# Four graph layers on one core: the value products stand ahead of the ring step in TensorE's program

## The reference

```python
# layers 0 and 1: one head; layer 2: eight heads, with types of edges
e = leaky_relu(s_src[:, :, None] + s_dst[:, None, :]);  e = where(adj > 0, e, NEG_BIG)
h_prime = einsum('bij,bjf->bif', softmax(e), h)          # the "value product"
...
# layer 3: for each pair of nodes a sum over 64 features
s = u[:, :, None, :] + v[:, None, :, :];  s = where(s > 0, s, ALPHA * s)
e = einsum('bijf,f->bij', s, a[:, 0])
h_prime = einsum('bij,bjf->bif', softmax(where(adj > 0, e, NEG_INF)), hp)
```

## Time and profile before

| | |
|---|---|
| median of three runs | 8730.86 us (8719.59 to 8737.53) |
| the profiled execution: its time | 8735.48 us |
| its span, first to last instruction | 8733.7 us |
| busy share of PE, DVE, ACT, POOL | 90%, 87%, 85%, 18% |
| mean granted TensorE clock | 0.975 of full speed |

### The profile page before, as it was taken

One profiled execution on the slowest core, in us unless ns is written; L12 is line 12 of the kernel. 1 busy time (PEld: TensorE's weight loads), 2 busy tenths in 40 slices (PEclk: granted clock), 3 DMA queues, 4 the chain that ended last, 5 costly groups with the idle time before them and its releaser, 6 DMA issues. The chain is left out here.

```text
span 8733.7 us, 176152 instructions
## 1 busy us (share of the span) xinstructions
PE 7856.0 (90%) x64968; PEld 3583.3 (41%) x64968; DVE 7563.2 (87%) x10853; ACT 7430.4 (85%) x8671; POOL 1535.9 (18%) x582
## 2 busy tenths in 40 slices
PE   4789999898989989999898898989999899898998
PEld 2535344353443534334343343534435344353442
DVE  4789888888889888898888898888888888988888
ACT  3688898988889888898888888889898898988888
POOL 0310304012040220302104030030301304012000
PEclk8999999999999999999999999999999999999999
DMA  3626344362443625335253352534526344362430
GB/s 86 162 56 140 78 108 113 73 144 66 112 104 83 142 64 115 96 87 139 65 122 97 84 135 59 126 91 96 124 58 143 77 108 112 76 143 67 109 83 19
DMA packets 519909, 864.90 MB, mean 99 GB/s; under 512 B 91938, under 2 KB 157474, under 8 KB 518946
## 3 DMA queue, kind: packets, MB, share of 16 engines
q1 hardware_dynamic: 518946, 852.41, 41.5%
HBM read 76.25 MB, written 4.19 MB: 9 GB/s over the span
## 5 line engine op out<-in xcount | busy, mean ns | idle before, releaser
L1134 ACT ACTIVATE work<-v,ucol 128x1024 f32<-128x1024 f32 x3757 | 4059.8, 1141 | 468.9 <-PE psum L879 466.6
L879 PE MATMUL psum<-work,pick 128*32 128x512 f32 x32768 | 3956.7, 609 | 342.5 <-DVE work L1471 208.4
L1471 DVE TENSOR_SCALAR work<-v,ucol 128x1024 f32<-128x1024 f32 x4435 | 3410.9, 823 | 204.4 <-PE psum L879 181.7
L879 PEld LDWEIGHTS psum<-work,pick 128*32 128x32 f32 x32768 | 938.2, 110 | 2601.7 <-issue 2238.1
L1281 DVE CUSTOM_DVE_ANT_0 work<-psum,work 128x1024 f32<-128x1024 f32 x1280 | 1542.5, 1205 | 320.0 <-ACT work L992 292.1
L1309 DVE STREAM_TRANSPOSE work<-work 128x1024 f32<-128x1024 f32 x1280 | 1582.7, 1237 | 56.9 <-DMA work<-work 56.2
L992 ACT ACTIVATE work<-psum,beta 128x1024 f32<-128x1024 f32 x1024 | 1138.9, 1112 | 429.8 <-PE psum L754 382.9
L1001 ACT ACTIVATE work<-work,least 128x1024 f32<-128x1024 f32 x1280 | 1463.2, 1143 | 18.9 <-DVE least L1281 18.8
L792 PEld LDWEIGHTS psum<-work,vw 128*64 128x64 f32 x16384 | 877.4, 137 | 613.2 <-issue 603.0
L792 PE MATMUL psum<-work,vw 128*64 128x128 f32 x16384 | 1118.8, 279 | 8.4 <-DMA work<-work 8.4
L750 PE MATMUL psum<-mask_next,ident_b 128*128 128x512 bf16 x2560 | 783.7, 388 | 337.0 <-DVE least L1281 306.1
(11 more groups left out here) (158 smaller groups left out, 5191.8 us busy)
## 6 DMA issues: line engine op xcount, KB each, us to landing
work<-work SPq DMA_DIRECT2D x2560, 256.0 KB, 4.6
adj_in<-in_adj SPq DMA_DIRECT2D x128, 512.0 KB, 3.6
tile3T<-blocks SPq DMA_DIRECT2D x512, 128.0 KB, 2.7
mask<-mask_next SPq DMA_DIRECT2D x128, 256.0 KB, 3.8
x_in<-in_x SPq DMA_DIRECT2D x16, 256.0 KB, 4.7
xT_both<-in_xT SPq DMA_DIRECT2D x16, 256.0 KB, 5.8
out<-yout SPq DMA_DIRECT2D x16, 256.0 KB, 2.6
work<-in_WqT SPq DMA_DIRECT2D x1, 128.0 KB
```

The source lines that it names most:

```text
L879: mm = pe.matmul(score3[32 * q:32 * q + 32, cols], pick[:, 15 - kk:47 - kk], ring[u % RING][q][:, cols], start=(kk == 0), stop=(kk == 15), ...
L1134: ins = act.activation(ring[u % RING][q], v3[:], ACT.Relu, bias=ucol[:, 4 * T + q, kk:kk + 1])
L1471: ins = dve.tensor_scalar(ring[u % RING][q], v3[:], ucol[:, 4 * T + q, kk:kk + 1], 0.0, ALU.add, ALU.max)
```

## The change

In PE's program the value product of a slot is taken out of `ahead` and called before the ring step. Nothing is added or removed, and the other engines' programs are as they were.

```diff
-            def ahead(a, it, s):
+            def products(a, it, s):
                 if s in PV_AT:
                     k, half = PV_AT[s]
                     if half is None:
                         pv_pair(a, it, k)
                     else:
                         pv_heads(a, it, k, half)
+
+            def ahead(a, it, s):
                 if s == 2:
                     column(a, it, 0)
...
                     if more and s in Q_AT:
                         make_q(g + 1, it, Q_AT[s])
+                    if more:
+                        products(g + 1, it, s)
                     if kk is not None:
                         ring_step(g, 16 * T + kk)
                     if s == 1:
...
                     make_q(0, first, Q_AT[s])
+                products(0, first, s)
                 ahead(0, first, s)
```

## The result

The change makes the kernel slower: 8781.32 us, the median of 5 runs (8768.48 to 8791.93), against 8732.98 us for the kernel before on the same chip (5 runs, 8719.59 to 8737.93). The ratio is 1.0052, with a 95% interval of 1.0037 to 1.0067. That is +48 us where +66 us was forecast, or 3.2 us a pass instead of 4.4. The profiled execution took 8777.45 us.

The account below looks back on a forecast made before the run. The prediction took a PE-DVE chain as the bound: a tile's last ring step, DVE's top read and queue, then PE waiting. Terms of 1.88 + 1.0 + 1.03 + 0.5 = 4.4 us, times 15, gave 66 us: 8799 us, range 8755 to 8830.

Parts of the forecast that it names:

- The last step of the sum: Shift from 8801 us, based on the profiled execution, to the median of runs, 4.6 us lower; given as 8799.
- Slot 15, 1.88 us: P0 ahead of R15 delays the top read; DVE's full queue passes 1.88 us a pass on to R27.
- a rival in which longer waits lower PE's clock: Added waits before R48 and R27 bring one more low-clock spell a pass, 1.68 us: 8824 us; chance 0.08.
- Slots 45 to 48, 1.0 us: P5 no longer covers the read after R47; R48 late, less about half the wait won before R45: 1.0 us.
- my bound of 1.32: Slots 45 to 48: R48 1.32 us late if nothing of the 0.48 us wait is won.
- Slots 119 to 127, 1.03 us: Half a product more ahead of R95 delays the top read; busy DVE passes 1.03 us on to S71.
- Slots 136 to 144, 0.5 us: Half products ahead of R104 to R109, partly filling R106's wait; R111 and its top read come 0.5 us later.
- The bound of 0: Slots 136 to 144: lower end of that term's range, 0 to 1.03 us a pass.
- Transfers, 0: Products wanting their pairs earlier cost nothing; at most 2 us a pass, on PE only, from tight pairs.
- The signs: Idle before reads 3.96 towards 5.8 and 2.33 to 3.4 us; R48 waits 1.7, R27 1.2 more; pass 538 us.
- PE's share alone: DVE catches up behind slots 15 and 119, so only PE's delay counts: 2.2 us a pass, 8768 us; chance 0.18.
- The products fill PE's waits: Products fill waits before R45, R47 and R106; 1.4 us a pass won, faster kernel at 8713 us; chance 0.06.

Follow-up runs that it names:

- only15: Kernel before with only the product of slot 15 (P0) moved ahead of its ring step; 8760.91 us, ratio 1.0027.
- noends: Kernel before with all products ahead of their ring steps except those of slots 15, 47, 119 and 143; 8742.83 us, ratio 1.0010.
- pull15: Kernel before with the values of layer 3 (8 matmuls) moved from ahead of R15 to behind it; 8677.93 us, ratio 0.9932.
- p0andpull: Kernel before with the values of layer 3 moved behind R15 and P0 moved ahead of R15; 8693.70 us, ratio 0.9956.
- best: Kernel before with layer 3's values behind R15 and the products of slots 136 to 142 and 144 ahead of their ring steps; 8678.26 us, ratio 0.9934.
- only47: Kernel before with only the product of slot 47 (P5) moved ahead of its ring step; 8759.19 us, ratio 1.0025.
- waits: Kernel before with only the products of slots 45, 136 to 142 and 144 moved ahead of their ring steps; 8727.20 us, ratio 0.9990.
- only119: Kernel before with only the second half of P28 (slot 119) moved ahead of ring step R95; 8758.24 us, ratio 1.0023.

## Why the prediction was right, and where it was off

The mechanism held: what stands ahead of a tile's last ring step delays the top read, and DVE's queue hands it on. The direction is right, 48 us lie 18 below the 66 forecast, and the four terms, measured one by one, give 22 + 20 + 20 + 0 = 62 us. Each of these is known to some 8 to 10 us and the 48 to some 13, so 62 and 48 aren't told apart. Some of the closeness is luck: the term of slot 119 got its size by a path that the sum didn't have, and the last term was nothing. The last step of the sum has a slip of 2 us: 8801 less 4.6 is 8797, not 8799.

*Slot 15, 1.88 us.* Right up to R27. In the change R27 moves by 1.81 us against R14 (1.21 + 0.60), and its row is 30.58 us behind the read. What followed was missed: at R32 only 1.06 us were left. R29 and the product behind it had been the place of low-clock spells, 1.65 us in 6 of 14 passes, 0.7 us a pass; after the change there is not one in 14. I had a rival in which longer waits lower PE's clock. At this place it went the other way: R29's wait is 1.71 us after, 2.02 before, and the clock stays up. The spells of R15 (8 of 14 passes) moved to P0 (6 of 14), and new ones came at R42 (4 passes). The mean clock is nearly the same, 0.976 and 0.975, and the time at the low clock went from 431 us to 421, so the clock is no cause of the 48 us. In only15, with R29's wait at 2.02 us, five spells stayed and the pass kept 2.1 us. It is not the chance of one execution: in the five traces in which R29 waits 1.82 us or less on average (the change, noends, pull15, p0andpull, best) no spell covers R29 in any of 14 passes, and in the nine in which it waits 1.86 to 2.03 us it is 4 to 8 of 14. Why, isn't shown.

*Slots 45 to 48, 1.0 us.* Mis-sized. The change gave 1.36 us from R43 (+0.66) to R52, beyond my bound of 1.32, and only47 1.4 (1.23 + 0.16). I had credited half of the wait before R45. None of it is won: waits shows it come back before R46 and R47, since the units are late and not PE.

*Slots 119 to 127, 1.03 us.* The size was about right, 20 us measured against 15, and its step wrong. "DVE is busy for 23.68 of 23.90 us, up to 4607.9": my window ended where DVE's wait for a transfer begins, 0.80 us up to 4608.83 in that pass. With it DVE had slack, and the delay shrank to 0.42 us in only119. It came back by longer ring units, which I hadn't in the sum.

*Slots 136 to 144, 0.5 us.* The size at R114 was 0.8 to 0.9 us: 0.25 is P38's wait for its transfers, and a ring step that is followed by another one takes 1.74 us, followed by a product 1.86, which parts R110 and R111 now. The cost is none within 8 us; by the table 0.6 us of it is gone between R114 and R127, where PE waits for DVE. The bound of 0 was the right value. I had not followed the pass beyond R111.

*Transfers, 0.* Right for the change as a whole. It was right because other delays covered them; noends uncovered 1.5 us.

*The signs.* The idle times of 5.8 and 3.4 us came as written, and R48's wait of 1.8; a pass took 536.3 us instead of 538. R27's wait grew by nothing instead of 1.2 us: a wait appeared at R23, 0.70 us, so the delay reached PE there first.

The rival "PE's share alone" is excluded by only15. "The products fill PE's waits" gains nothing at R45 by the table of waits, and little at R106: 9 us in all.

## What to carry to other kernels

In two engines that hand work back and forth, the place of an operation matters by what waits for the step behind it. Put nothing ahead of the step whose end the other engine is idle for, and keep something behind it to cover the reply; moving one 8-matmul operation that way paid 0.7%, moving many the wrong way cost 0.5%. When a stretch is called full, let the window run until the waiting step itself, and follow the pass to its end for idle time that takes a delay up. And test both signs: at slot 119 a delay cost 20 us, and an advance paid nothing.

## What the hardware showed that I had not expected

GpSimd's additions make DVE's ring units longer: 0.75 us alone, 2.31 on average and up to 2.63 beside the one for the mask. Cutting 408 us of additions (2.28 us x 120 and 1.40 us x 96) to 62 took 141.9 us from the busy time of DVE's ring units and 137 us from the kernel's. The Trainium skill ("SBUF — State Buffer", section "SBUF: two separate sides") says that DVE and GpSimd share one pair of ports, and that a GpSimd instruction and a DVE instruction of certain kinds (a performance mode that uses both ports, or two inputs in SBUF) block each other: the first to start holds the pair for its whole length. No run here shows in which mode the ring units work. For the additions the trace agrees. For GpSimd's two conversions of the mask (L1590, L1591), 3.93 us each, it doesn't fit: the 565 ring units that overlap most with one of them take 1.06 us on average and 1.59 at most. What the trace shows beyond the rule is the price of the additions in this kernel, 1.5% of the time, at an engine that is busy for only 18% of the span.

The spells of low clock cover the same few steps in many passes (R15, R29, P0, R42), cost about 1.65 us each there, and appear and vanish there with changes of the order by one operation. Over a run they came to much the same number in the two kernels, 73 before and 69 after, and to 58 in pull15.
